# Mixture-of-experts stage: eight in-place weight buffers, loads tied to a scatter count

## What is computed

```python
x = x + attn(layernorm(x))           # linear attention, 2048 tokens, width 512
x = x + moe(layernorm(x))
# moe: 32 routed experts (+32 "zero" experts), 8 of 64 chosen per token
scores = softmax(xf @ w_cls.T);  topk of scores + bias;  w = weights of the chosen, scaled
gu  = einsum('ech,ehf->ecf', buf, w_gate_up)    # per expert 512 -> 512
act = silu(g) * u
y   = einsum('eci,eih->ech', act, w_down)       # per expert 256 -> 512
out[token] += w * y                              # for each chosen routed expert
```

## Time and profile before

| what | value |
|---|---|
| median of 3 runs | 1019.9 us (1015.76 to 1022.46) |
| the profiled execution's own time | 1025.01 us |
| its span, first to last instruction | 1023.2 us |
| experts block within the span | from 740 us to the end |
| busy, whole span | PE 88%, DVE 75%, ACT 49%, POOL 48% |
| GpSimd's scatters | 38, first at 768.41 us, last at 1010.94 us |

### The profile page before, as it was taken

The page is one execution under the profiler, slowest core; times in us unless marked ns, Lnnn a source line. Parts: engine busy times, 40 slices in busy tenths (PEclk is TensorE's granted clock), DMA queues, the critical chain, the costliest instruction groups (busy, mean ns, idle before and its releaser), DMA issues. The chain is left out here.

```text
span 1023.2 us, 14443 instructions
## 1 busy us (share of the span) xinstructions
PE 905.2 (88%) x4313; PEld 731.7 (72%) x4313; DVE 771.3 (75%) x1837; ACT 503.7 (49%) x867; POOL 495.9 (48%) x420
## 2 busy tenths in 40 slices
PE   5789999999999999999699999999379897687960
PEld 3577888888888888888488888888357575566740
DVE  6978888888888888888777777776768767485720
ACT  5455555555555554555642333332258766475730
POOL 2456676666667666666400000000065566656652
PEclk9989999999999999999999999999679989797985
DMA  8001111111111111103755654431189979798743
GB/s 295 6 32 47 57 41 53 47 57 42 58 47 57 37 58 47 56 33 104 264 171 184 254 184 146 145 105 54 44 287 280 321 218 283 212 276 235 184 61 41
DMA packets 52758, 131.01 MB, mean 128 GB/s; under 512 B 12156, under 2 KB 14588, under 8 KB 46528
## 3 DMA queue, kind: packets, MB, share of 16 engines
q1 hardware_dynamic: 41248, 114.67, 32.4%
q0 software_dynamic: 11424, 15.29, 8.6%
HBM read 106.53 MB, written 35.91 MB: 139 GB/s over the span
## 5 line engine op out<-in xcount | busy, mean ns | idle before, releaser
L595 POOL TENSOR_TENSOR a_t<-a_t 128x512 f32<-128x512 f32 x80 | 105.2, 1315 | 101.7 <-DVE a_t L358 101.7
L1081 DVE TENSOR_TENSOR w_l<-raw,w_h 128x1024 fp32r<-128x1024 f32 x96 | 114.7, 1222 | 13.5 <-ACT w_h L1074 13.2
L604 POOL TENSOR_TENSOR a_fQ<-a_fQ,a_den 128x512 f32<-128x512 f32 x64 | 88.0, 1376 | 71.8 <-DVE a_den L396 71.8
L213 PE MATMUL a_PQ<-w_h,a_xT_h 128*128 128x512 f32 x384 | 107.8, 403 | 10.0 <-DVE w_l L345 9.3
L775 PE MATMUL r_PY<-w_h,r_o_h 128*128 128x512 f32 x256 | 106.3, 415 | 3.4 <-DVE r_o_l L867 3.4
L1179 POOL DMA_INDIRECT out<-m_y,si x38 | 66.2, 1741 | 88.0 <-DMA out<-m_y,si 64.5
L1051 POOL TENSOR_SCALAR r_vr<-r_mv 128x1 f32<-128x1 f32 x16 | 8.4, 526 | 199.0 <-DVE r_mv L878 199.0
L213 PE MATMUL a_PQ<-w_l,a_xT_h 128*128 128x512 f32 x384 | 104.2, 394 | 0.0
L213 PE MATMUL a_PQ<-w_h,a_xT_l 128*128 128x512 f32 x384 | 103.5, 392 | 0.0
L775 PE MATMUL r_PY<-w_l,r_o_h 128*128 128x512 f32 x256 | 101.9, 398 | 0.0
L775 PE MATMUL r_PY<-w_h,r_o_l 128*128 128x512 f32 x256 | 101.8, 398 | 0.0
(11 more groups left out here) (168 smaller groups left out, 2193.8 us busy)
## 6 DMA issues: line engine op xcount, KB each, us to landing
raw<-in_wgu SPq DMA_DIRECT2D x32, 1024.0 KB, 6.8
oT<-a_o SPq DMA_DIRECT2D x64, 256.0 KB, 2.5
raw<-in_wd SPq DMA_DIRECT2D x32, 512.0 KB, 6.4
v_l<-oT SPq DMA_DIRECT2D x11, 1024.0 KB, 6.6
v_h<-oT SPq DMA_DIRECT2D x5, 1024.0 KB, 6.7
out<-r_x SPq DMA_DIRECT2D x18, 256.0 KB, 2.0
a_xin<-in_x SPq DMA_DIRECT2D x16, 256.0 KB, 3.2
v_l<-in_wq SPq DMA_DIRECT2D x4, 1024.0 KB, 12.4
```

The costliest lines, as they stand in the source:

```text
L213: last = eng.matmul(bank[:, :], a[:, k, :], w[:, 4 * i + k, :], start=s == 0 and k == 0, stop=s == 2 and k == 3)
L595: eng.tensor_tensor(t1[:, r % 2, :], t1[:, r % 2, :], t2[:, r % 2, :], ALU.add).then_inc(sm["xr"], 1)
L604: eng.tensor_tensor(q, q, den[:, n % 2, :].unsqueeze(2).broadcast_to([P, 4, P]), ALU.mult).then_inc(sm["fs"], 1)
L1081: eng.tensor_tensor(low, src, high.bitcast(F32), ALU.subtract).then_inc(sm["m_wl"], 1)
```

## The change

- A ring of eight raw buffers takes the place of three. Three lie where the raw buffers lay, four where `w_l` lay, the eighth in a free piece of `w_h`'s memory and one of its own. Low parts are written over the raw weights in place (`parts`), so a buffer is free only when the expert's matmuls are done.
- The host lays the weights out as [4, 128, 512] and [2, 128, 512]. Each load is still 1 MB or 0.5 MB, now in rows of 2 KB.
- Experts 0 to 2 and the up weights of expert 7 are loaded in routing's chunks 2 to 5; experts 3, 4 and 5 at its end, around the last `store_w`; expert 6 and the down weights of 7 in the experts block, once gathers of experts 0 and 1 have landed.
- From expert 8 on SP loads expert e when the count `m_sent` says that GpSimd has issued the scatter of expert e-8.
- The small transfer `m_spare` and its branch are gone: a first-half scatter without a second adds 32 to the one semaphore `m_s`. The flag is read and the branch taken before the wait for landings, which is now inside it. Gathers of second halves no longer wait for the gather six experts before.
- PE: in iteration 0 up(0) comes before turn(1). DVE clears all six buffers first. ACT waits for the identity matrix after its first two splits. SP, not GpSimd, waits for the last landing.

```diff
+    up, _, _, _ = ring[e % RING]
+    eng.dma_start(up, wgu[e].rearrange("k p f -> p k f")).then_inc(sm[f"m_wg{e % RING}"], 16)
...
+                    if c == 5:
+                        load_up(sm, eng, ring, wgu, 7)
...
+                eng.wait_ge(sm["r_y"], NC)
+                for e in (3, 4):
+                    load_up(sm, eng, ring, wgu, e)
+                    load_down(sm, eng, ring, wd, e)
                 store_w(NC - 1)
+                load_up(sm, eng, ring, wgu, 5)
+                load_down(sm, eng, ring, wd, 5)
...
-                for e in range(3, NE):
-                    eng.wait_ge(sm["m_wl"], 3 * (e - 3) + 2)
-                    eng.dma_start(raw[e % 3][:, 0:4, :], wgu[e]).then_inc(sm[f"m_wg{e % 3}"], 16)
-                    eng.wait_ge(sm["m_wl"], 3 * (e - 3) + 3)
-                    eng.dma_start(raw[e % 3][:, 4:6, :], wd[e]).then_inc(sm[f"m_wd{e % 3}"], 16)
+                load_up(sm, eng, ring, wgu, 6)
+                load_down(sm, eng, ring, wd, 6)
+                eng.wait_ge(sm["m_g11"], 16)
+                load_down(sm, eng, ring, wd, 7)
+                for e in range(RING, NE):
+                    eng.wait_ge(sm["m_sent"], e - RING + 1)
+                    load_up(sm, eng, ring, wgu, e)
+                    load_down(sm, eng, ring, wd, e)
+                eng.wait_ge(sm["m_s"], 32 * NE)
...
-                    no_scatter(e)
                     if e + 6 < NE:
                         gather(e + 6, 0)
                         gather(e + 6, 1)
-                    scatter(e, 0)
+                    load_flag(eng, regs, e)
                     with eng.If_lt(regs[e % 7], T):
-                        scatter(e, 1)
+                        scatter(e, 0, 16)
+                        scatter(e, 1, 16)
+                        eng.sem_inc(sm["m_sent"], 1)
+                    with eng.Else():
+                        scatter(e, 0, 32)
+                        eng.sem_inc(sm["m_sent"], 1)
...
+                    if e == 0:
+                        both(eng, regs, 0, up, "m_gu1")
                     both(eng, regs, e + 1, turn, "m_xt1")
-                    both(eng, regs, e, up, "m_gu1")
+                    if e > 0:
+                        both(eng, regs, e, up, "m_gu1")
...
-        "wgu": np.asarray(L0_ffn_w_gate_up).reshape(NE, 4, P, 512).transpose(0, 2, 1, 3),
+        "wgu": np.asarray(L0_ffn_w_gate_up).reshape(NE, 4, P, 512),
```

More of the change, by code:

```diff
@@ L628, in _, with routing @@
                         rstd(c + 1)
-def routing(nc, sm, x, wo, wc, bias, consts, oT, xn2d, out, gi, si, raw, wgu, wd, w_h_, w_l_, v_h, v_l):
+def routing(nc, sm, x, wo, wc, bias, consts, oT, xn2d, out, gi, si, ring, wgu, wd, w_h_, w_l_, v_h, v_l):
     with ExitStack() as ctx:
@@ L967, in _ @@
                     else:
-                        split_low(sm, eng, raw, w_h_, w_l_, 0, 0)
+                        split_low(sm, eng, ring, w_h_, 0, 0)
                     xT_low(c)
@@ L973, in _ @@
                     else:
-                        split_low(sm, eng, raw, w_h_, w_l_, 0, 1)
+                        split_low(sm, eng, ring, w_h_, 0, 1)
                     choose(c)
@@ L977, in _ @@
                     slots(c)
-                split_low(sm, eng, raw, w_h_, w_l_, 0, 2)
+                split_low(sm, eng, ring, w_h_, 0, 2)
                 eng.wait_ge(sm["r_tbl"], NC)
@@ L1026, in _ @@
                         eng.wait_ge(sm["r_y"], NC)
-                        split_high(sm, eng, raw, w_h_, 0, 0)
-                        split_high(sm, eng, raw, w_h_, 0, 1)
+                        split_high(sm, eng, ring, w_h_, 0, 0)
+                        split_high(sm, eng, ring, w_h_, 0, 1)
                     eng.wait_ge(sm["r_xt"], c + 1)
@@ L1033, in _ @@
                     if c == NC - 1:
-                        split_high(sm, eng, raw, w_h_, 0, 2)
+                        split_high(sm, eng, ring, w_h_, 0, 2)
                     eng.wait_ge(sm["r_nm"], c + 1)
@@ L1056, in _, with load_up, load_down, pair @@
                     rstd(c)
-def part_of(raw, w, e, part):
-    if part < 2:
[L1063 to L1069, removed]
+RING = 8
+def load_up(sm, eng, ring, wgu, e):
+    up, _, _, _ = ring[e % RING]
+    eng.dma_start(up, wgu[e].rearrange("k p f -> p k f")).then_inc(sm[f"m_wg{e % RING}"], 16)
+def load_down(sm, eng, ring, wd, e):
+    _, down, _, _ = ring[e % RING]
+    eng.dma_start(down, wd[e].rearrange("k p f -> p k f")).then_inc(sm[f"m_wd{e % RING}"], 16)
+def pair(ap):
+    return ap.rearrange("p k t -> p (k t)")
+def parts(ring, w_h, e, part):
+    up, down, up_l, down_l = ring[e % RING]
+    if part < 2:
+        i = 4 * (e % 3) + 2 * part
+        k = slice(2 * part, 2 * part + 2)
+        return pair(up[:, k, :]), pair(w_h[:, i:i + 2, :]), pair(up_l[:, k, :])
+    i = 12 + 2 * (e % 4)
+    return pair(down), pair(w_h[:, i:i + 2, :]), pair(down_l)
+def split_high(sm, eng, ring, w_h, e, part):
     if part != 1:
         kind = "m_wd" if part == 2 else "m_wg"
-        eng.wait_ge(sm[f"{kind}{e % 3}"], 16 * (e // 3 + 1))
-    src, high = part_of(raw, w_h, e, part)
+        eng.wait_ge(sm[f"{kind}{e % RING}"], 16 * (e // RING + 1))
+    src, high, _ = parts(ring, w_h, e, part)
     eng.activation(high, src, ACT.Copy).then_inc(sm["m_wh"], 1)
-def split_low(sm, eng, raw, w_h, w_l, e, part):
+def split_low(sm, eng, ring, w_h, e, part):
     eng.wait_ge(sm["m_wh"], 3 * e + part + 1)
-    src, high = part_of(raw, w_h, e, part)
-    src, low = part_of(raw, w_l, e, part)
+    src, high, low = parts(ring, w_h, e, part)
     eng.tensor_tensor(low, src, high.bitcast(F32), ALU.subtract).then_inc(sm["m_wl"], 1)
-def experts(nc, sm, wgu, wd, xn2d, out, gi, si, raw, consts, w_h, w_l):
+def experts(nc, sm, wgu, wd, xn2d, out, gi, si, ring, consts, w_h, w_l, v_h):
     with ExitStack() as ctx:
@@ L1101, in experts @@
         y = sb("y", [P, 4, 2, D])
-        spare = sb("spare", [1, 2, 16])
+        with nc.sbuf_tensor("m_raw", [P, 2, 512], F32) as raw:
+            pass
+        low = sb("low", [P, 2, 512], F32R)
         ident = sb("ident", [P, P])
@@ L1108, in experts @@
         PY = [ps("PY0"), ps("PY1")]
+        ring = ring + [(v_h[:, 20:24, :], raw[:, :, :], w_h[:, 20:24, :], low[:, :, :])]
         def f(ap):
@@ L1163, in gather, with scatter @@
                         bounds_check=T - 1, oob_is_err=False).then_inc(sm[f"m_g{t}{e % 6}"], 16)
[L1165 to L1173, removed]
+                def scatter(e, t, done):
                     i = 2 * e + t
                     if t == 0 and e >= 1:
-                        eng.wait_ge(sm["m_s0"], 16 * e)
-                        eng.wait_ge(sm[f"m_s1{(e - 1) % 2}"], 16 * ((e + 1) // 2))
+                        eng.wait_ge(sm["m_s"], 32 * e)
                     eng.wait_ge(sm[f"m_y{t}"], e + 1)
@@ L1180, in scatter @@
                         out[:, :], bass.IndirectOffsetOnAxis(ap=si[:, i:i + 1], axis=0),
-                        y[:, e % 4, t, :], None, compute_op=ALU.add).then_inc(sm["m_s0" if t == 0 else f"m_s1{e % 2}"], 16)
+                        y[:, e % 4, t, :], None, compute_op=ALU.add).then_inc(sm["m_s"], done)
                 for e in range(6):
@@ L1218, in up @@
                         eng.wait_ge(sm["m_wl"], 3 * e + 2)
-                    steps = [(xT_h, w_h), (xT_h, w_l), (xT_l, w_h)]
+                    high, low_ = w_h[:, 4 * (e % 3):4 * (e % 3) + 4, :], ring[e % RING][2]
+                    steps = [(xT_h, high), (xT_h, low_), (xT_l, high)]
                     for i, (x_, w_) in enumerate(steps):
                         for k in range(4):
-                            last = eng.matmul(PG[t][:, :], x_[:, e % 2, t, k, :], w_[:, 4 * (e % 3) + k, :],
+                            last = eng.matmul(PG[t][:, :], x_[:, e % 2, t, k, :], w_[:, k, :],
                                               start=i == 0 and k == 0, stop=i == 2 and k == 3)
@@ L1239, in down @@
                         eng.wait_ge(sm[f"m_y{t}"], e)
-                    steps = [(a_h, w_h), (a_h, w_l), (a_l, w_h)]
+                    high, low_ = w_h[:, 12 + 2 * (e % 4):14 + 2 * (e % 4), :], ring[e % RING][3]
+                    steps = [(a_h, high), (a_h, low_), (a_l, high)]
                     for i, (a_, w_) in enumerate(steps):
                         for b in range(2):
-                            last = eng.matmul(PY[t][:, :], a_[:, t, b * P:(b + 1) * P], w_[:, 12 + 2 * (e % 4) + b, :],
+                            last = eng.matmul(PY[t][:, :], a_[:, t, b * P:(b + 1) * P], w_[:, b, :],
                                               start=i == 0 and b == 0, stop=i == 2 and b == 1)
@@ L1262, in w_low @@
                         for part in parts:
-                            split_low(sm, eng, raw, w_h, w_l, e, part)
+                            split_low(sm, eng, ring, w_h, e, part)
                 def x_low(e, t):
@@ L1283, in clear @@
                     eng.memset(xg[:, i, 1, :], 0.0).then_inc(sm["m_xg"], 1)
-                clear(0)
-                clear(1)
```

(15 more changed lines are left out.)

18 lines of the change are left out of this document (5 added, 13 removed).

## The result

| | before | after |
|---|---|---|
| median | 1018.82 us (4 runs) | 1045.55 us (4 runs, 1041.03 to 1045.87) |
| ratio | 1 | 1.025, 95% interval 1.021 to 1.030 |
| span of the profiled execution | 1023.2 us | 1043.5 us |

The change made the kernel 2.5% slower. I had forecast 984 us and a range up to 1006. All medians in this document leave out one slow execution, of the kernel with the count by work and PE's first order (1139.1 us, at a granted clock of 0.74 where its other three show 0.96 to 0.97).

What follows compares the result with a forecast made beforehand. Bound: GpSimd's scatter chain, from issue to landing. Intervals of 51.6 + 126.0 + 27.9 = 205.5 us against 242.5 gave -37.0, the start +1: 1019.9 - 36.0 = 983.9, say 984 us (972 to 994; with rivals (a) to (c), 966 to 1006).

Steps and rivals of the forecast that it cites:

- The bound: Experts block: GpSimd's chain of scatters holds PE and ACT, through the time from issue to landing; 242.5 us for 31 intervals.
- The small transfer's removal: GpSimd in the experts block: own work falls from 5.6 to about 4.9 us per expert, 0 us on the path.
- Early loads: Loads of 5.8 MB moved ahead of the experts block: 16 us of DMA work out of it, no delay from `store_w`.
- Weights were never waited for: Loads from expert 8 on: 12 us of lag is less than their lead, so almost no ACT wait for weights.
- Rows of 2 KB: Scatters beside loads: shorter load rows free the engines sooner, landing after 6.3 us instead of 9.12.
- eight turns: A scatter's 8 rows per engine each wait for one load row: 2.9 us with 8 KB rows, 0.7 with 2 KB.
- rival (a): Experts block: arithmetic becomes the bound, landing at 5.6 us or less as loads start behind the scatter; 969 us, chance 0.13.
- (e): Loads in many short rows are slow, ACT waits for weights and DMA sets the pace; +61, 1045 us, chance 0.08.
- (b): Scatters beside loads: the load holds an engine for 16 rows, 1.4 us; landing 7.0, 998 us, chance 0.13.
- Start: Start of experts block: up(0) ends 3 us earlier, silu(0) moves to about 759, 3 us later; +1 us taken.
- End: From the last scatter's issue to program end: 12.3 us, only who waits for the landing changes; 0 us.
- Sum: Scatter intervals take 205.5 us against 242.5, -37.0; with the start -36.0, giving 984 us.

Runs made afterwards that it cites:

- count by work: The changed kernel with the count raised by a one-element GpSimd write queued behind the scatter, not by its program: 988.9 us, ratio 0.972.
- count by work and PE's first order: The count by work kernel with expert 1's rows again turned ahead of expert 0's up matmuls, as before the change: 984.1 us, ratio 0.965.
- changed, long rows: The changed kernel with weights laid out and loaded in rows of 8 and 4 KB as before: 1028.4 us, ratio 1.010.
- changed, no late loads: The changed kernel without the 24 loads from expert 8 on, so its results are wrong: 970.0 us, ratio 0.954.
- write without count: Control: the changed kernel with a one-element GpSimd write behind the scatter, but the count raised where it was: 1041.8 us, ratio 1.023.

## Why the prediction was wrong

**Right.** The bound (GpSimd's scatter chain, and in it the landing) was read rightly, and it was still the bound after. Loads in its way were its cause: without late loads the interval is 5.84 us. The small transfer's removal gave nothing on the path, as said: GpSimd's own work fell by 1 us and its wait grew. Early loads disturbed nothing: the block began 1.1 us later, no more. Weights were never waited for.

**The step that failed** is "Rows of 2 KB", the landing at 4.93 + 0.7 + 0.65 = 6.3 us. It measured 8.94. The step put all of the load's price on the scatter's rows, one load row for each of them, and made that price fall with the row's length. The packets say where the time is (means of the 20, us from the scatter's start):

| kernel | first row | last row | interval |
|---|---|---|---|
| before | 3.7 | 7.3 | 8.20 |
| changed | 5.2 | 8.1 | 8.94 |
| changed, long rows | 5.0 | 7.7 | 8.45 |
| changed, no late loads | 2.3 | 4.4 | 5.84 |
| count by work | 2.9 | 5.9 | 6.75 |
| write without count | 5.2 | 8.1 | 8.94 |

Once they move, the rows of a scatter of the changed kernel take 2.9 us, and with the loads in long rows 2.7, against 2.1 without a load: less than 1 us for the turns, whatever the length, and 1.5 in the kernel before, where I had 2.9. The change's price lies ahead of the first row: 5.2 us instead of 2.3, a term that the sum did not have.

The step rested on the earlier trace rows, and that row does not show what I called it. Its software queue moved 0.49 MB in 3 us, and a whole scatter is 0.26 MB. By size 110 of the 162 packets are gather rows, 7 are the scatter's and 45 are packets of 4 bytes, as are 18 of the load's 155. Two queues that both have rows share the engines there, but it says nothing of a scatter that comes just behind a load. In the interval that I took apart, 841.49 to 850.61, the first row came after 3.95 us, 1.8 late, and the rows took 4.2 us, 2.1 longer than alone; 2.9 us for eight turns fitted by chance.

**What I read and did not use.** The change is to issue each load behind a scatter, and I counted that in its favour (rival (a): "the scatter gets a head start") without asking when a count raised by GpSimd's program comes. A scatter's instruction takes 1.6 us, a count does not wait for it, and SP answers at once (0.03 us after the write's end in the run with the count by work). In the kernel before, loads started with DVE's splits, at any moment of an interval; some scatters met none (882.40 us, an interval of 5.6), others two (910.01 us, with loads issued at 906.06 and 911.63, an interval of 11.9). After, each has one in front. The count took chance out, at a bad point.

**The rivals.** (e) named 1045 us and it was 1045.6, by luck and not for its reason: no engine waited for weights, and DMA was busy 75% of the time from 768 to 1004 us, less than the 85% of the earlier trace rows (81% in the same stretch of the kernel before):

```profile
768.00:1004.00 236.00, 192.49 (x814) 149.13 (x813) 151.54 (x185) 143.62 (x220) 113.42 (x81) 0.91 0.75 208
```

The mechanism that set the time, a load in front of every scatter, was in none of my cases. (b), long turns, was nearer: the Trainium skill (DMA: Bandwidth & Descriptors, "Queues, rings and completion order") has an engine drain a whole packet of one queue, typically 9 to 17 descriptors, before it switches. The 3 us by which the first row is late are twice the 16 short rows (1.4 us) that I had priced for it.

**Start.** I took +1 out of -3 to +3 for PE's order; from PE's first matmul of the block to the first scatter it was +5.3 in the profiled execution and about +3 in the other kernels with that order. I had silu(0) at 759 us. It came at 761.14, behind ACT's copies for turn(1) and two splits, and PE stood idle for it. PE's timeline, and the windows of the changed kernel and of the kernel before:

```profile
763.13 1.12 PE L1254 MATMUL m_PA<-m_ident,m_a 128*128 128x128 f32 x4 [6.09 <-DVE m_a L1301]
```

```profile
764.00:768.00 4.00, 4.00 (x14) 3.32 (x13) 3.24 (x6) 3.13 (x5) 2.47 (x2) 0.50 0.09 20
```

```profile
764.00:768.00 4.00, 4.00 (x19) 3.23 (x18) 1.92 (x4) 1.80 (x3) 0.28 (x1) 1.00 1.02 374
```

After the 6.1 us of idle time PE's granted clock is at its lower level, 0.50 (1.2 GHz), for up(1), where before it was 1.00. The sum had no term for that.

**End.** -3.2 us where I took 0.

**Sum.** Of the 36 us forecast, the 24 intervals with loads should have given 201.1 - 160.4, about 41; they cost 19.3 instead. With the count raised by work behind the scatter the forecast's interval (6.75 against 6.3 us) and time (988.9 against 984) come nearly true, by another way than row length.

**Open.** Why the software queue moves nothing while a load is in front isn't shown; whether the engines hold on to the load or the scatter's rows are made late beside it can't be told from these traces. It isn't the work of the other engines, which is there in the kernel without late loads too (2.3 us). One thing fits the first: in 23 of the changed kernel's 24 intervals at least 511 rows of the load had moved before the scatter's first row, and its 1 MB part has 512. Once the scatter's rows move, the load's share of the engines is not fixed: with the count by work it runs from 0 to 0.65, a third on average. Nor is it shown why rows of 2 KB make a load 0.9 us longer here, when their steady rate is as good.

## What to carry to other kernels

A semaphore raised by a program behind an asynchronous transfer says that the transfer was handed on, not that its rows move; where the order of two transfers matters, raise it by an instruction of work that queues behind the first, and look in the trace at which queue moves first. When a transfer is on the critical path and bulk loads are not, the moment of the loads can outweigh their size, their rows and the number of buffers: here some 2 us of delay were worth some 55 us. A share of packets read in one stretch is no rule for another in which one queue came first, and a row of a queue should be checked for whose packets it holds: bytes against the size of the transfer tell it.

## What the runs showed of the hardware

A scatter's rows start 2.1 to 2.2 us after its instruction does, with nothing in the way. A 1.5 MB load issued by SP 0.2 us ahead of it keeps them out until 4.9 to 6.0 us after its start, in rows of 2 KB, and 4.7 to 5.7 us in rows of 8 and 4 KB. Once they move, 128 rows take 2.1 us alone and 2.7 to 2.9 us beside a load. GpSimd's program raised a count 2.4 us before the start of the gather that stood ahead of it. Loads land after 6.2 us (1 MB, median of 32) in rows of 2 KB and after 5.3 us in rows of 8 KB.
